# Splitting the first FFN's sixteen sequences into groups of 3, 4, 4 and 5 in place of 4, 6 and 6 (one core)

## The reference

```
x = x + 0.5 * ffn(layernorm(x))       # the first FFN
x = x + attention(layernorm(x))
x = x + 0.5 * ffn(layernorm(x))       # the second FFN, the same weights
```

## The kernel before, in words

| group of | big units | quad units | units |
|---|---|---|---|
| 3 | 4 | 12 | 16 |
| 4 | 8 | 12 | 20 |
| 5 | 12 | 12 | 24 |
| 6 | 16 | 12 | 28 |

## Time and profile before

### The profile page before, as it was taken

One profiled execution on the slowest core, in us unless ns is written; L12 is line 12 of the kernel. 1 busy time (PEld: TensorE's weight loads), 2 busy tenths in 40 slices (PEclk: granted clock), 3 DMA queues, 4 the chain that ended last, 5 costly groups with the idle time before them and its releaser, 6 DMA issues.

```text
span 1808.6 us, 39999 instructions
## 1 busy us (share of the span) xinstructions
PE 1649.0 (91%) x12493; PEld 1264.2 (70%) x12493; DVE 1099.8 (61%) x3414; ACT 893.7 (49%) x1376; POOL 1041.6 (58%) x1186
## 2 busy tenths in 40 slices
PE   5757999889989999999999999899999989989998
PEld 4535777677767777787777787577777767867655
DVE  4786457664854456457556655557556576744775
ACT  6323445336565665465656656536656545433111
POOL 3477765777772337733464464363566767763760
PEclk9878999999999999999999999999999999999999
DMA  9547999799855659884765677474688889999440
GB/s 299 191 143 191 242 254 236 231 251 233 233 162 121 161 147 247 229 198 120 165 175 146 151 199 174 110 175 119 167 211 203 213 219 249 239 255 232 146 134 24
DMA packets 502897, 343.39 MB, mean 190 GB/s; under 512 B 333591, under 2 KB 471982, under 8 KB 502702
## 3 DMA queue, kind: packets, MB, share of 16 engines
q1 hardware_dynamic: 456434, 214.92, 48.7%
q0 software_dynamic: 46080, 125.89, 25.3%
q10 hardware_dynamic: 188, 0.03, 0.0%
HBM read 96.37 MB, written 168.82 MB: 147 GB/s over the span
## 4 chain that ended last, share of the span: by engine, by line
PE 41%; POOL 26%; issue 11%; DVE 10%; SPq 5%; DMA 5%; ACT 2%; DVEq 0%; POOLq 0%; ACTq 0%
POOL yg L1487 13%; POOL xd L1473 11%; PE bank L1135 7%; PE bank L988 5%; PE bank L990 4%; PE bank L989 4%; PE bank L1188 4%; SPq L962 3%; PE bank L1139 3%; DMA yg<-yd,idx 2%; PE bank L1078 2%; PE bank L1079 2%; PE bank L1083 2%; DVE xb L1766 2%; PE bank L1150 2%
## 5 line engine op out<-in xcount | busy, mean ns | idle before, releaser
L1473 POOL DMA_INDIRECT xd<-xs,idx x480 | 483.5, 1007 | 429.1 <-DVE picked L1627 221.9
L1487 POOL DMA_INDIRECT yg<-yd,idx x480 | 474.7, 989 | 178.5 <-issue 142.8
L988 PE MATMUL bank<-xtp,gu_hi 128*128 128x128 f16 (+1 forms) x1728 | 369.8, 240 | 26.2 <-DMA xtp<-xd 10.3
L989 PE MATMUL bank<-xtp,gu_hi 128*128 128x128 f16 (+1 forms) x1728 | 368.7, 239 | 0.0
L990 PE MATMUL bank<-xtp,gu_lo 128*128 128x128 f16 (+1 forms) x1728 | 367.8, 239 | 0.0
L1135 PE MATMUL bank<-dn,h 128*128 x1152 | 310.6, 393 | 30.3 <-DVE h L1727 16.8
L1342 ACT ACTIVATE ybuf<-bank 128x512 f32<-128x512 f32 x288 | 171.2, 595 | 295.2 <-PE bank L1135 262.5
L1727 DVE SCALAR_TENSOR_TENSOR h<-bank,h 128x512 f32<-128x512 f32 x240 | 165.5, 690 | 226.6 <-PE bank L990 146.1
L1335 ACT ACTIVATE h<-bank 128x512 f32<-128x512 f32 x240 | 141.9, 596 | 307.1 <-PE bank L1083 181.1
L1135 PEld LDWEIGHTS bank<-dn,h 128*128 128x128 f32 x1152 | 206.6, 193 | 72.5 <-issue 43.8
L1766 DVE SCALAR_TENSOR_TENSOR xb<-yg,comb,xb 128x256 f32<-128x256 f32 x480 | 195.3, 479 | 93.6 <-DMA yg<-yd,idx 93.6
(11 more groups left out here) (239 smaller groups left out, 2778.7 us busy)
## 6 DMA issues: line engine op xcount, KB each, us to landing
yd<-ybuf SPq DMA_DIRECT2D x144, 256.0 KB
yd<-ybuf SPq DMA_DIRECT2D x288, 128.0 KB
xr<-xb SPq DMA_DIRECT2D x30, 512.0 KB
xb<-xr SPq DMA_DIRECT2D x30, 512.0 KB, 5.1
xb<-in_attn_x_dram SPq DMA_DIRECT2D x16, 512.0 KB, 5.8
out_dram<-xb SPq DMA_DIRECT2D x16, 512.0 KB
xd<-xs,idx POOLq DMA_INDIRECT x480
yg<-yd,idx POOLq DMA_INDIRECT x480
```

The lines of the kernel that those rows point to most:

```text
L988: pe.matmul(out_ap, a_hi, b_hi, start=(i == 0), stop=False)
L989: pe.matmul(out_ap, a_hi, b_lo, start=False, stop=False)
L1473: pool.indirect_dma_start(out=xd[buffer_of[q]][:, :], out_offset=bass.IndirectOffsetOnAxis(ap=idx[:, r % SEQS, t, k:k + 1], axis=0), in_=x ...
L1487: pool.indirect_dma_start(out=yg[:, half, t % 2, j].bitcast(U32), out_offset=None, in_=yd[buffer_of[q]][:, :], in_offset=bass.IndirectOffs ...
```

## The change

Sequences 0 to 2 form the first group, 3 to 6 the second, 7 to 10 the third and 11 to 15 the fourth, in place of 0 to 3, 4 to 9 and 10 to 15.

```
-CHUNKS = ((4, 6, 6), (5, 5, 4))
+CHUNKS = ((3, 4, 4, 5), (5, 5, 4))
```

## The result

The changed kernel takes 1857.12 us (median of 3 runs, 1852.4 to 1862.86) against 1819.06. The ratio is 1.0209, with a 95% interval of 1.0151 to 1.0268: it is slower, by 38 us. I had forecast +6.5 us, and the upper end of the range was 1846. All its runs lie between 1809.34 and 1831.91 us, a spread of 1.2%, so the "some tenths of a per cent" at the top are too few.) The profiled execution has a span of 1850.5 us, 41.9 more than before.

What follows compares the result with a forecast made beforehand. PE was taken as the bound after the first units begin. Terms +19.5 (units) + 3 (table) + 0 - 10 (early start) - 6 (attention) = +6.5 us gave 1825.5 us, 8-in-10 range 1800 to 1846.

Steps and rivals of the forecast that it cites:

- The early start: First group closes a sequence earlier, units begin near 139.4 us, PE's loss from 134 to 161 us shrinks: 10 us gained.
- More units: First FFN gets 12 more quads and 8 fewer big units: +19.5 us of PE work, ends 14 and 24.
- SP and DMA at nothing: Added loads and stores, +51 us on SP and 17.5 us on DMA, costed at nothing because PE is filled meanwhile.
- Attention begins earlier: First gather some 60 us earlier, removing PE gaps from 161 to 550 us: 6 us gained, ends -4 and 8.
- The table and the fourth region: One more table chain on DVE, +3 us; one more 2 MB zeroing write at the start, 0 us.
- Rival 2: Feed by DMA and SP becomes the bound, PE waits for `xtp` between 161 and 480 us: 1844.5 us, chance 0.19.
- Rival 1: Early attention removes a third of PE's 56 us idle between 550 and 1600 us: 1807 us, chance 0.19.
- Rival 3: No early start: planned order or DVE's table keeps the first unit where it is: 1835.5 us, chance 0.11.
- Rival 4: Weight loads set the quads' matmul pitch at 98 ns in place of 56, 24 us more: 1850 us, chance 0.04.
- The signs for the whole: If right, over the whole kernel PE is busy about 15 to 20 us more and idle about 15 less.

Runs made afterwards that it cites:

- the added units: Kernel before with four empty but executed quad units more in the first FFN (1, 1 and 2 in its groups): 1856.47 us, ratio 1.0183.
- The hold alone: Changed kernel with the attention of sequence 4 held until 54 units are stored: 1844.5 us, ratio 1.0137.
- the groups of 3, 6 and 7: Kernel before with first-FFN groups of 3, 6, 7 sequences, no added unit or table: 1842.6 us; with sequence 3's attention held until unit 49 is stored, 1810.87 us.
- the groups of 4: Kernel before with first-FFN groups of 4, 4, 4 and 4 sequences, 80 units, seven tables, no early start: 1878.06 us, ratio 1.0316.
- half the issues: Changed kernel, quads among the last 32 units issue two of their four transposing loads: 1837.43 us, ratio 1.0113.
- half the rows: Changed kernel, quads among the last 32 units issue all four loads with 64 rows each in place of 128: 1853.75 us, ratio 1.0190.

## Why the prediction was wrong

- **The early start: right in size, in part by luck.** Units begin at 141.8 us where 139.4 was worked out. By the forecast's own measure PE's loss between 134 and 161 is 27 - 20.48 x 0.81 = 10.4 us where it was 13.7; the ledger's loss up to 161 us falls by 5.0 and up to 550 us by another 5.8, 10.8 together; taken back, the early start costs 9.7 us. The 10 us stand, but only 3 to 5 of them come between 134 and 161, where I had put them all; the rest comes up to 550 us, which I had counted again as the 6 us of the earlier attention. For the two steps together I had taken 16 us, and up to 550 us 10.8 came.
- **More units: the count right, one part misread.** The 1344 matmuls per line are there. But each unit has two downs, and each of them is the four records of 0.87 us in the earlier trace rows; I took one. That is 1.74 us in place of 0.87, so 12 - 8 = 4 more units cost 3.5 us more than I said. Against it I took a quad's `up` at 1.74 us, with gaps in it; at 56 ns the 48 matmuls are 2.7 us, the quad 2.7 + 1.7 = 4.4 and the big unit 2.6 + 1.7 = 4.35: 12 x 4.4 - 8 x 4.35 = +18.0. The ledger measures +18.5. So the +19.5 was right to a microsecond because two errors cancel. The 1152 matmuls at L1135 for 144 units would have told me.
- **SP and DMA at nothing: the step that failed.** I had the right numbers (+51 us on SP, 6.7 us a quad there against 4 on PE) and costed them at nothing "because PE is filled there with shared units, routing and then attention", and called that the cover on which the sum depends. The cover is a fixed amount of work. The new order uses it up earlier: `residual` of sequence 15 ends at 1521 in place of 1577 us, and with it gone 28 units in place of 12 run at SP's 7 us each. PE's loss after 1400 us is 30.1 us larger, of which some 24 lie in that stretch. The experiments put the added units at 9.1 us each, of which 4.4 is PE. How much of the difference is SP's issue and how much the order stays open.
- **Attention begins earlier: the wrong sign.** I bounded the step at -8 and +4 by what happens up to 550 us only. An attention that starts earlier also ends earlier, and what is late then is the units. No term of the sum looks at when the attention is over. The hold alone, which undoes this, is worth 12.6 us here and 32 in the groups of 3, 6 and 7. The first gather came at 351.6 us, not near 300 (365.5 before), so even the way there was read wrongly. The sixteen units of the first group are through at 301 us, 14 us behind the 287 worked out; POOL then still had the scatters of sequences 10 and 11 and the first of 12 ahead of the gather in its order, and takes the gather up without a wait:

```profile
351.59 1.07 POOL L1487 DMA_INDIRECT yg<-yd,idx  x1 [0.30 <-issue]
```

- **The table and the fourth region:** seven tables were made; nothing in the profile of after stands out at the seventh, and its 3 us were not tried by themselves. (Some 30 instructions of 0.2 us are 6.0 us, not 6.5; nothing hangs on it.) The zeroing lands in 10.2 us as before.
- **The rivals.** Rival 2 named the feed, and its mark, PE's waits on `xtp<-xd`, did pass 10 us. But that was at the end and not between 161 and 480 us, where I put it. From 1518 to 1715 us in the profile after (total, times, longest):

```profile
PE bank L988 <- DMA xtp<-xd: 10.7, 9, 2.4
```

  From 134 to 560 us the same wait sums to 5.5 us, and 3.0 before. So rival 2 as written, and its price of 19 us, is not what happened; it had the right queue at the wrong end of the kernel. Rival 1 is out: the loss from 550 to 1400 us went up by 4.3 us in all, and PE's idle time from 550 to 1600 us, its own mark, from 56.0 to 70.3 us. Rival 3 is out by the 141.8 us. Rival 4 is out: up to 200 us the matmuls of L988 have the median length of before, with 94 of 128 columns among them in place of 48, and their start-to-start pitch has a median of 56 ns in the whole of after too:

```profile
L988 PE MATMUL bank<-xtp,gu_hi x110: 216/219/421, 141.8 to 199.4; 128*128 128x128 f16 x94, 128*128 128x256 f16 x16
```

- **The signs for the whole:** PE was to be busy 15 to 20 us more and idle some 15 less. It was busy 29.1 us more, some of it at the lower clock, and idle 12.8 us more (159.6 to 172.4).

Still open: how the 9.1 us of an added unit divide between SP's issue and the planner's other order (every added unit gives a new one); why the order of groups of 3, 6 and 7 costs 32 us; whether a hold would make the kernel before faster too; what the seventh table costs alone; and the 11 us of the groups of 4.

## What to carry to other kernels

Work that hides a slow feed is a budget that gets used up: when a change lets that work run ahead, ask how many of the units that it covered are left when it is over, and what they cost at the pace of their own queue. Where an order comes from a list scheduler, a change of group sizes is also a change of order, which here was worth up to 32 us with the same work; try the sizes in several orders before judging them. And price a unit by adding an empty one: it shows at once what a sum over its matmuls misses.

## What the runs showed of the hardware

- A transposing load holds SP's queue for about 1.2 us and hardly more for more rows: 1170 ns with 64 rows, 1189 with 128, 1234 with 256. A plain store takes 0.35 to 0.39 us there. Where that queue bound, halving the issues of 18 quads took 20 us off and halving their bytes 3.
- A DMA share of 1.01 over 115 us was not a bound: with less to move it fell to 0.88 and no time came of it.
- Where PE had waited for its feed at the end, its granted clock averaged 0.79 over 30 us (1620 to 1650); with half the issues it was 1.00 from 1600 to 1650. With half the rows, which takes no issue away, it averaged 0.96 from 1600 to 1715 in place of 0.93. So a slow feed may cost twice; one pair of traces doesn't prove it.
- A down in f32 appears as two matmuls per weight tile in the trace, at 216 ns each for 256 columns, where the code has one: L1135 has 8 records per unit and the code four calls. Counts of f32 matmuls by line have to be halved.
